# Gate and up products of a gated feed-forward as one 2x2 block product in seven products instead of eight, on one core

## The reference

```python
xn = _layernorm(x, axis=-1)
# attention, per row: q 32 heads x 16, k and v 8 heads x 16
q = einsum('bse,edh->bsdh', xn, Wq) + bq            # k, v alike, then repeated 4 times
scores = einsum('bsdh,bseh->bsde', q, k) / sqrt(16) # 16 x 16 per row
s = einsum('bsde,bseh->bsdh', softmax(scores), v)
# feed-forward
nx = xn * rsqrt(mean(xn * xn) + 1e-5) * ln_w
g = nx @ gate_w.T ;  u = nx @ up_w.T                # 1792 columns each
f = (silu(g) * u) @ down_w.T
out = x + s * silu(f)
```

## Time and profile before

| What | Value |
|---|---|
| Median of 3 runs | 522.2 us |
| Profiled execution, first to last instruction | 520.4 us |
| TensorE busy | 507.2 us, 97% |
| VectorE busy | 374.8 us, 72% |
| ScalarE busy | 195.1 us, 37% |
| GpSimd busy | 27.5 us, 5% |
| Moved by DMA | 33.1 MB |
| Granted TensorE clock, mean | 0.997 |

### The profile page before, as it was taken

The page is one execution under the profiler, slowest core; times in us unless marked ns, Lnnn a source line. Parts: engine busy times, 40 slices in busy tenths (PEclk is TensorE's granted clock), DMA queues, the critical chain, the costliest instruction groups (busy, mean ns, idle before and its releaser), DMA issues.

```text
span 520.4 us, 6685 instructions
## 1 busy us (share of the span) xinstructions
PE 507.2 (97%) x2320; PEld 424.8 (82%) x2320; DVE 374.8 (72%) x542; ACT 195.1 (37%) x373; POOL 27.5 (5%) x41
## 2 busy tenths in 40 slices
PE   6999999999999999999999999999999999999993
PEld 5888888888888888888888888888888888888882
DVE  6899756876278653886569797686775867588777
ACT  4857862124311234114276575211332114221311
POOL 5030010200102000010000000000000000000000
PEclk9999999999999999999999999999999999999998
DMA  8823350000400004000043212201031010300312
GB/s 269 287 82 102 97 186 0 1 1 2 161 0 0 0 0 161 0 0 0 0 161 102 81 42 81 82 0 40 0 128 74 0 40 0 122 0 1 112 50 81
DMA packets 15168, 33.11 MB, mean 64 GB/s; under 512 B 1456, under 2 KB 2736, under 8 KB 14384
## 3 DMA queue, kind: packets, MB, share of 16 engines
q1 hardware_dynamic: 13200, 22.42, 13.5%
q0 software_dynamic: 1952, 10.49, 5.8%
HBM read 25.56 MB, written 7.34 MB: 63 GB/s over the span
## 4 chain that ended last, share of the span: by engine, by line
PE 95%; DVE 2%; ACT 1%; DMA 1%; SPq 0%; issue 0%; DVEq 0%; ACTq 0%
PE gate_ps L283 29%; PE up_ps L283 29%; PE y_ps L283 29%; PE aux_ps L283 6%; PE aux_ps L367 1%; DMA raw<-gate 1%; DVE raw L702 1%; DVE y_part L697 0%; ACT zT_hi L536 0%; DVE y_part L687 0%; SPq L172 0%; ACT raw L437 0%; DVE h_lo L746 0%; DVE h L738 0%; ACT y_part L526 0%
## 5 line engine op out<-in xcount | busy, mean ns | idle before, releaser
L471 ACT ACTIVATE h_hi<-h 128x512 fp32r<-128x512 f32 x56 | 35.4, 632 | 173.9 <-DVE h L738 159.4
L738 DVE TENSOR_TENSOR h<-h,up_ps 128x512 f32<-128x512 f32 x56 | 38.4, 687 | 79.4 <-PE up_ps L283 76.8
L283 PE MATMUL y_ps<-down_hi,h_hi 128*128 128x512 f32 x224 | 88.4, 395 | 0.3 <-DVE h_lo L746 0.3
L283 PE MATMUL y_ps<-down_hi,h_lo 128*128 128x512 f32 x224 | 87.7, 391 | 0.0
L283 PE MATMUL up_ps<-zT_hi,up_hi 128*128 128x512 f32 x224 | 87.5, 391 | 0.0
L283 PE MATMUL y_ps<-down_lo,h_hi 128*128 128x512 f32 x224 | 87.5, 390 | 0.0
L283 PE MATMUL up_ps<-zT_hi,up_lo 128*128 128x512 f32 x224 | 87.3, 390 | 0.0
L283 PE MATMUL up_ps<-zT_lo,up_hi 128*128 128x512 f32 x224 | 87.2, 389 | 0.0
L283 PE MATMUL gate_ps<-zT_hi,gate_hi 128*128 128x512 f32 x224 | 83.3, 389 | 1.0 <-ACT zT_hi L536 1.0
L283 PE MATMUL gate_ps<-zT_hi,gate_lo 128*128 128x512 f32 x224 | 83.3, 389 | 0.0
L283 PE MATMUL gate_ps<-zT_lo,gate_hi 128*128 128x512 f32 x224 | 83.3, 389 | 0.0
(11 more groups left out here) (75 smaller groups left out, 603.2 us busy)
## 6 DMA issues: line engine op xcount, KB each, us to landing
z<-x POOLq DMA_DIRECT2D x4, 1024.0 KB, 6.9
raw<-x SPq DMA_DIRECT2D x4, 1024.0 KB, 5.5
out<-raw SPq DMA_DIRECT2D x16, 256.0 KB, 2.0
raw<-gate SPq DMA_DIRECT2D x14, 256.0 KB, 2.7
raw<-up SPq DMA_DIRECT2D x14, 256.0 KB, 2.7
raw<-down SPq DMA_DIRECT2D x14, 256.0 KB, 2.7
zT_kept<-zT_raw POOLq DMA_DIRECT2D x3, 1024.0 KB, 8.5
zT_raw<-zT_kept POOLq DMA_DIRECT2D x3, 1024.0 KB, 5.1
```

What stands on the lines that cost most here:

```text
L283: last = pe.matmul(acc, lhsT, rhs, start=start and n == 0, stop=stop and n == len(pairs) - 1)
L471: act.activation(h_hi[:, i % 2, :], h[:, i % 2, :], ACT.Copy).then_inc(h_hi_done, 1)
L738: dve.tensor_tensor(h[:, i % 2, :], h[:, i % 2, :], up_ps[:, i % 2, :], ALU.mult)\
```

## The change

**The seven products.** The four weight parts (gate and up, each with its first and second half of K) are a 2x2 block matrix A, and the transposed rows of two blocks (each with its first and second half of K) a 2x2 block matrix B. The four results (gate and up of block 0, gate and up of block 1) are made by Winograd's form of Strassen's scheme. Each of the 7 products is 2 chunks of K by 3 matmuls, so 6 matmuls of 512 columns, 42 for a group (one step of 128 hidden units for a pair of blocks) where before there were 48. The factors `WS1` to `WS4` are sums of weight parts, `ZT1` to `ZT4` sums of parts of B, each with its own high and low part.

The core of the diff (what is left out is the rest of the lists, the tiles and the semaphores):

```diff
+            def product(acc, g, m, start=False):
+                wi, zi = m
+                for c in range(2):
+                    w_h, w_l = (w_ops[:, g % 2, s, wi, c * P:(c + 1) * P] for s in range(2))
+                    pe.matmul(acc, w_h, z_hi[:, zi, c, :], start=start and c == 0, stop=False, ...
+                    pe.matmul(acc, w_h, z_lo[:, zi, c, :], start=False, stop=False, skip_group_check=True)
+                    end = pe.matmul(acc, w_l, z_hi[:, zi, c, :], start=False, stop=c == 1, ...
...
+            for g in range(NI, GROUPS):
+                m1(g)
+                m5(g)
+                m6(g)
+                m2(g)
+                m7(g)
+                down_product(g + NI - 1)
+                m4(g)
+                m3(g)
...
+            def down_tile(u, j):
+                blk, n = item(u)
+                if n == 0 and u:
+                    if blk == 0 or u < 2 * NI:
+                        pe.wait_ge(y_done, J * (u // NI - 1) + j + 1)
...
+            def h_lo_part(u):
+                blk, n = item(u)
+                pool.wait_ge(h_hi_done, u + 1)
+                wait(pool, d_done, J * (u - 1))
+                src = h_kept[:, n, :] if blk else h0[:, n % 2, :]
+                pool.tensor_tensor(h_lo[:, u % 2, :], src, h_hi[:, u % 2, :].bitcast(F32), ALU.subtract)
...
+            def seed(g):
+                act.wait_ge(m1_done, g + 1)
+                if g >= 2:
+                    act.wait_ge(c12_done, g)
+                act.activation(gu_ps[:, bank_b(g), :], gu_ps[:, bank_a(g), :], ACT.Copy).then_inc(seeded, 1)
...
+            def take_u2(g):
+                act.wait_ge(m6_done, g + 1)
+                wait(act, h1_done, g)
+                act.activation(u2[:], gu_ps[:, bank_a(g), :], ACT.Copy).then_inc(u2_done, 1)
...
+            silu1(NI - 1)
+            h_hi_part(NI)
+            for j in range(3):
+                z_hi_tile(1, j)
+                if j:
+                    z_raw_tile(1, j - 1)
+            for j in range(3, JJ):
+                z_raw_tile(1, j - 1)
+                z_hi_tile(1, j)
+            z_raw_tile(1, JJ - 1)
+            for j in range(J):
+                y_out(0, j)
+            for u in range(NI + 1, 2 * NI):
+                h_hi_part(u)
...
+                attention(shares[g][0])
+                c22(g)
+                attention(shares[g][1])
+                if g == NI + 6:
+                    for j in range(J):
+                        finish(1, j)
+                times_up0(g)
```

More of the change, by code:

```diff
@@ L166, in build, with scores_end, values_end @@
+        STEPS = 13 * PAIRS * JJ
+        places = [attn_place(q) for q in range(STEPS)]
+        def scores_end(pair):
+            return places.index((False, 2 * pair + 1, 5)) + 1
+        def values_end(tile):
+            return places.index((True, tile, 6)) + 1
         block = ctx.enter_context(nc.Block())
@@ L214, in _ @@
+            for u in range(ITEMS - NI, ITEMS):
+                load_wd(u)
+                if u == ITEMS - 6:
+                    store(2)
+                    load_fin_x(3)
+            store(3)
+            sp.wait_ge(fin_stored, 16 * J * 4)
         @block.gpsimd
@@ new lines, in _ @@
+            for g in range(NI, GROUPS):
+                seed(g)
+                if g > NI:
+                    silu1(g - 1)
+                if g == NI + 1:
+                    for j in range(J):
+                        y_out(1, j)
+                take_u2(g)
+                silu0(g)
+                take_u3(g)
+                if g > NI:
+                    exps(exps_in(g))
+                if g == LAST:
+                    h_hi_part(2 * NI + NI - 1)
+                h_hi_part(item_of(1, 0, g - NI))
@@ new lines, in _, with attention, finish @@
+            taken = [0]
+            def attention(steps):
+                for _ in range(min(steps, STEPS - taken[0])):
+                    values, tile, step = places[taken[0]]
+                    wait(dve, attn_step, taken[0])
+                    (attn_values if values else attn_scores)(tile, step).then_inc(attn_step, 1)
+                    taken[0] += 1
+            def finish(f, j):
+                tile = J * f + j
+                dve.wait_ge(y_done, tile + 1)
+                dve.wait_ge(attn_step, values_end(tile))
+                y3 = fin_y[:, j, :].rearrange("p (s r) -> p s r", r=REP)
+                s = attn[:, tile, :].unsqueeze(2).to_broadcast([P, DG, REP])
@@ L807, in _ @@
[L807 to L821 removed]
+                z_lo_tile(0, j)
@@ new lines, in _ @@
+            first_tiles(J, between)
+            lo_a(0, 2, 3, 3)
+            sums(0)
+            qkv_take(0)
+            z_lo_tile(0, J)
+            z_lo_tile(0, J + 1)
+            qkv_take(1)
+            z_lo_tile(0, J + 2)
+            z_lo_tile(0, J + 3)
+            lo_s(0)
+            qkv_take(2)
+            for n in range(4):
+                t_add(0, n)
+            qkv_take(3)
+            for n in range(3):
+                t_lo(0, n)
+                qkv_take(4 + n)
+            lo_a(1, 2, 3, 4)
@@ L824 @@
+            c12(LAST)
+            times_up1(LAST)
+            attention(values_end(3 * J - 1) - taken[0])
+            for j in range(J):
+                finish(2, j)
+            attention(STEPS)
+            for j in range(J):
+                finish(3, j)
 def kernel(L0_attn_x, L0_attn_Wq, L0_attn_bq, L0_attn_Wk, L0_attn_bk, L0_attn_Wv, L0_attn_bv,
```

1324 lines of the change are left out of this document (770 added, 554 removed).

## The result

The changed kernel is slower: a median of 535.3 us (531.1 to 536.1, 4 runs) against 522.2 (521.9 to 522.4, 4 runs), a ratio of 1.023 with a 95% interval of 1.020 to 1.027. The profiled execution has a span of 534.2. The forecast was 519.2, faster than before by 3.0, with a range of 504 to 534. The runs of one kernel differ by up to 6 us, and the start alone takes up to 2 us more in one profiled execution than in another that shares it, so stages are compared inside the profiled executions.

The account below looks back on a forecast made before the run. TensorE, busy 97% of the span, was taken as the bound: 477.8 without waits, plus waits 16.3 + 10.2 + 4.0 + 4.3 + 4.8, gave a span of 517.4 us; with 1.8 to the median, 519.2, range 504 to 534.

Parts of the forecast that it names:

- The waits of the start: Before group 2, TensorE waits 16.3 us, with a gap of 4 near 21 us and two of 3 before 45.
- Groups 2 to 13: First pair's twelve groups: M7 waits 3.0 us in all, 1.0 if GpSimd disturbs nothing, 5.5 if subtractions hold VectorE throughout.
- GpSimd's subtraction: Making a low part of 512 columns on GpSimd takes 1.2 us, chosen between 0.69 and 1.7.
- the loop that hides it up to 1.7: In down-product runs, 0.2 + 0.63 + 0.05 + subtraction + 0.15 against 2.72 us: no cost up to a 1.7 subtraction.
- one wait over 5 us, ended by `y_out`: Between the pairs, down product 14 waits 5.7 us for y_out(0), part of 10.2 us of waits there.
- The sign that the prediction named for this case: For the clock case: a granted clock under 0.9 in a window between the pairs.
- Both are hidden: 0.: Transfers in first-pair and second-pair groups finish within the group and cost 0 us.
- After the run, 4.0: Behind the run between the pairs, VectorE about 2 us late: c22(14) and seed(15) cost 2.0 + 1.4, y_out(1) 0.6.
- Group 20's `finish(1)`, 4.3: In group 20, finish(1) adds 5.5 us to VectorE, slack takes 1.2, leaving a wait of 4.3.
- The tail and the small gaps: Behind the last matmul 5.4 us; small gaps behind the q, k, v products 0.9 us.
- Rival 3: GpSimd's subtractions and VectorE's two-SBUF-operand instructions exclude each other, in groups and last runs: 539 us, or 529 at half; chance 0.23.
- Rival 4: TensorE's clock falls to 1.2 GHz between the pairs and at the start: 2 to 10 us lost, 521 to 529; chance 0.10.

Follow-up runs that it names:

- e11_best: e9_hlo and e10_last together; 509.8 us, ratio 0.975.
- e1_fill: The changed kernel with matmuls whose results are unused put into TensorE's waits at the start and between the pairs; 530.3 us, ratio 1.016.
- e7_twice: e5_all with GpSimd making each low part of h twice, one after the other; 548.1 us, ratio 1.051.
- e2_tail: The changed kernel with block 2's store and the load of block 3's x moved behind the last down weights in SyncE's queue; 531.9 us, ratio 1.018.
- e5_all: The changed kernel with the start's fillers, e3_yout, e4_spread, block 2's store two items earlier and x loaded in four pieces; 514.0 us, ratio 0.986.
- e10_last: e6_wdlo with the last item's high and low parts of h in a place of their own; 511.2 us, ratio 0.978.
- e6_wdlo: e5_all with the 14 low parts of the down weights made by VectorE, not GpSimd; 512.5 us, ratio 0.982.
- e9_hlo: e6_wdlo with the first pair's 14 low parts of block 0's h made by VectorE too; 513.1 us, ratio 0.982.
- e12_aside: e6_wdlo with 27 more GpSimd subtractions of constant tiles into a spare one, which nothing waits for; 522.8 us, ratio 1.001.
- e3_yout: The changed kernel with block 0's y_out interleaved with the second pair's tiles 4 to 7 and h_hi(15) made early; 530.4 us, ratio 1.016.
- e8_tadd: e6_wdlo with the first pair's four T additions at the start made by GpSimd, not VectorE; 513.3 us, ratio 0.985.
- e4_spread: The changed kernel with finish(1) dealt over groups 20 to 23, a tile each, and its store and next x load four groups later; 528.7 us, ratio 1.014.

## Why the prediction was wrong

**Right.** The seven products save their 38.1 us; with e11_best's waits the whole list runs in 508.8. The waits of the start: with the clock nearly full (e1_fill) group 2 begins at 70.4, forecast 70.2. Groups 2 to 13: 3.0 of waits forecast and 3.1 found, and "1.0 if GpSimd disturbs nothing" is nearly what e11_best has (148.0 against 12 x 12.24 = 146.9). GpSimd's subtraction: 1.2 forecast, 1.26 to 1.30 where VectorE is not in its way (1.56 in the mean in the runs of down products), and the loop that hides it up to 1.7 is borne out by e7_twice. (By the Trainium skill, page GPSIMD Engine Reference, section "Performance versus the Vector engine", 1.1 was estimated; the trace's 1.30 decides.) Between the pairs one wait over 5 us, ended by `y_out`.

**The step that failed first: the clock at nothing.** The forecast priced waits by their length, and had the clock only as a rival of its own, 0.10, though it forecast a wait of 5.7 and 16 us of waits at the start, and the earlier trace rows showed the clock fallen after 5 us without matmuls. It should have been a term: 6.0 at the start (e1_fill); 2.3 between the pairs, where the down product that begins at 241.9 takes 5.0 and not 2.72; 2.5 in group 21, which is 19.8 less 12.2 and 5.0 of wait from matmul to matmul; 2.5 in the last run, where the item that begins at 510.7 takes 5.2. Together 13.3 of a miss of 16.8 in the span. The sign that the prediction named for this case, a clock under 0.9 in a window between the pairs, is there with 0.62. The Trainium skill, page TensorE: Matmul & The Clock Gate, section "The HAM clock gate", has the rule that an idle engine is throttled; the trace agrees, with a clock of 0.86 in the wait of 505.7 to 510.7 and 0.50 behind it.

**The second: the transfers, "Both are hidden: 0."** It was worked out for groups alone. In the last run the store of block 2 (1 MB) and 1 MB of x stand ahead of 0.5 MB of weights in SyncE's queue. That costs twice. SyncE issues x only when the store has landed (503.10), so the weights are issued at 503.55, 6.5 behind those before them and not 2.7; and they land 7.0 later, behind x, where the ones before took 3.1 to 3.5. The result is 4.9 of wait, and the 2.5 of low clock behind it. e2_tail and e5_all show that the queue's order is the cause, and that putting it elsewhere has a price at the end.

**The third: `h_lo` of the last item.** The loop that makes GpSimd free holds while an item may use the other buffer. The last two items are run tile by tile, so both must be ready before either begins, and the last one's buffer is free only when the item two before is done: 0.2 + 0.63 + 0.05 + 1.3 + 0.15 = 2.3, and 2.32 came. e10_last takes it away.

**Terms that were mis-sized.** "After the run, 4.0": groups 14 and 15 took 12.29 and 12.24, so nothing; VectorE was busy 55.7 of the run's 70.9 and not behind TensorE. Group 20's `finish(1)`, 4.3: 5.0 of wait and 2.5 of low clock. These cancel, and groups 14 to 27 came out at 180.3 for 180.7 by that luck. The tail and the small gaps were 0.9 too high each. At the start the waits are 3.9 ahead of the first q, k, v product, 2.8 and 1.1 before 48 us, for a 4 and two of 3. Their sum can be set beside the forecast only where the clock is near full: in e1_fill group 2 begins 57.1 behind M1 with 40.5 of work between, so 16.6 went to waits and fillers, for 16.3.

**The rivals.** Rival 3, that the two engines exclude each other, has the right mechanism, and I gave it a price of 12 to 24 us. Three experiments show the mechanism: e6_wdlo and e9_hlo by taking the overlap away, e12_aside by adding some that nobody waits for. The Trainium skill, page SBUF — State Buffer, section "Who interferes with whom", says that the shared port pair is an exclusive lock; the traces agree, with VectorE's instruction ending 0.29 behind GpSimd's. But its price in the changed kernel's first-pair groups is 2.0 us (150.0 against 148.0 in e11_best). A first-pair group has two of GpSimd's subtractions; one costs VectorE 0.25 (L923), the other 0.76 (L907 and L908), and most of that goes into slack. With less slack left it costs more: 10 us in the median for 27 more, about half of the 19.0 by which VectorE's busy time grew; a first-pair group with one more is 0.57 longer. Rival 4, the clock, happened, but on top of the forecast's waits and not in their place, and for more than its 2 to 10 us.

**What stays open.** e3_yout won 4.1 between the pairs, less than the 2.3 of clock and 2.8 of shorter waits together; no run splits what took the rest. How long a wait must be to lower the clock is not shown: the transposes and waits of 0.8 to 1.2 between the pairs left it full in e3_yout, e5_all and e12_aside, and not in e6_wdlo, e8_tadd, e9_hlo, e10_last and e11_best (the last section has two windows). What the two engines' exclusion costs in the runs of down products is not shown either, since no run takes it away there. How long the start takes differs by 2 us between runs that share it; no run tells why.

## What to carry to other kernels

Taking matmuls away from this kernel, which TensorE bounds, left three waits of 5 us, and each cost about half its length again in matmuls at the lower clock. Before the products are counted as saved, break such a wait into pieces of 1 us (which brought the clock's loss to between 0 and 0.8 us here) or put matmuls in it. Check every place where the regular pattern ends (the last run, the last items) for what stands ahead in the queue and for which buffer comes free when; the steady state hides neither. Work that is moved to GpSimd to free VectorE is only free where VectorE has, at that moment, nothing with two operands in SBUF, or has slack.

## What the hardware showed beyond what was expected

- A wait of 4.9 us was followed by 5.3 us at 1.2 GHz with TensorE busy all the time; waits of 0.8 to 1.2 us left the clock at full in e3_yout and e4_spread, and so did the wait of 2.3 in the last run.
- The length of one wait alone does not tell whether the clock falls. In the changed kernel it was at 0.50 all through the wait between the pairs (236.50 to 241.90), and at 0.83 and 0.87 in the mean of the other two. Behind a wait of 2.07 at the start of e1_fill it was 0.55 for 3.8 us, behind one of 3.11 between the pairs of e7_twice 0.50 for 4.3 us. Between the pairs, TensorE has small transposes with waits of about 1.2 and then the waits of 0.8 to 0.9; there the clock fell in e6_wdlo, e8_tadd and e10_last (hidden in waits for ScalarE) and in e9_hlo and e11_best (0.8 us lost). Windows of e6_wdlo and e11_best:

```profile
228.00:231.50 3.50, 3.50 (x11) 2.60 (x9) 1.20 (x3) 2.97 (x7) 0.00 (x0) 0.58 0.43 142
...
233.00:236.00 3.00, 2.60 (x7) 1.59 (x6) 2.59 (x2) 1.66 (x3) 2.54 (x2) 0.50 0.34 98
```

- 30 matmuls of 128 columns whose results are never used made the start 6.0 us shorter (at least 3.3, by the nearest pair of starts with and without them).
- VectorE's instructions with one operand in PSUM (686 ns) and its reductions (1218 ns) kept their length beside 27 more of GpSimd's instructions; those with two in SBUF that begin inside one are held until it has ended (128x256: 0.42 to 1.52 us). The loss is mutual: GpSimd's `h_lo` behind VectorE's additions of 1024 columns took 2.25 us, at its shortest 1.26.
